# Window attention in units of two images by 64 queries on all 128 rows, with the last four queries of each image apart

## Reference, cut to what matters

```python
    q = (x @ Wq + bq).reshape(B, S, H, hd).transpose(0, 2, 1, 3)
    k = (x @ Wk + bk).reshape(B, S, H, hd).transpose(0, 2, 1, 3)
    v = (x @ Wv + bv).reshape(B, S, H, hd).transpose(0, 2, 1, 3)
    scale = 1.0 / jnp.sqrt(jnp.asarray(hd, x.dtype))
    scores = jnp.einsum('bhqd,bhkd->bhqk', q, k) * scale
    i = jnp.arange(S)[:, None]
    j = jnp.arange(S)[None, :]
    allowed = (j <= i) & (i - j < WINDOW)          # WINDOW = 64
    scores = jnp.where(allowed, scores, NEG_INF)
    attn = jax.nn.softmax(scores, axis=-1)
    out = jnp.einsum('bhqk,bhkd->bhqd', attn, v)
    out = out.transpose(0, 2, 1, 3).reshape(B, S, D)
    return out @ Wo + bo
```

## Time and profile before

| | |
|---|---|
| median of the runs | 1058.24 us |
| the profiled execution | 1058.27 us |
| its span, first to last instruction | 1056.5 us |
| mean granted TensorE clock | 0.961 |
| attention, first scores to last weigh | 54.95 to 222.66 us |
| units in it | 64 |

### The profile page before, as it was taken

How to read it: one execution, slowest core, us unless ns; L and a number is a source line. 1 busy time by engine, 2 the same in 40 slices (tenths; PEclk the granted TensorE clock), 3 DMA queues, 4 the chain that set the end, 5 groups by cost and what they waited for, 6 DMA issues and landing times. The chain is left out here.

```text
span 1056.5 us, 29782 instructions
## 1 busy us (share of the span) xinstructions
PE 950.1 (90%) x10440; PEld 746.9 (71%) x10440; DVE 589.3 (56%) x1463; ACT 412.9 (39%) x1102; POOL 522.1 (49%) x714
## 2 busy tenths in 40 slices
PE   8899999988747999999999999889979947999996
PEld 6667777777634888888888876445546635888895
DVE  1878888865994777433333325678877552111111
ACT  2266776634253344444444422223323222433331
POOL 0056655610604777776777627777773002433332
PEclk9999999999979999999999999989889987999998
DMA  7010000002004988877788723334482046486750
GB/s 257 1 46 2 0 0 0 2 11 75 1 1 165 307 275 254 277 243 224 242 264 255 228 88 100 101 115 120 121 288 82 22 182 228 143 271 215 266 155 26
DMA packets 79821, 149.30 MB, mean 141 GB/s; under 512 B 18892, under 2 KB 53327, under 8 KB 75760
## 3 DMA queue, kind: packets, MB, share of 16 engines
q1 hardware_dynamic: 34768, 77.15, 21.5%
q0 software_dynamic: 17712, 47.88, 15.8%
q10 hardware_dynamic: 27248, 23.09, 6.5%
HBM read 200.22 MB, written 31.73 MB: 220 GB/s over the span
## 5 line engine op out<-in xcount | busy, mean ns | idle before, releaser
L1332 POOL DMA_INDIRECT x_x<-m_x_rows,x_idx x170 | 166.1, 977 | 74.3 <-issue 35.8
L1358 PE MATMUL x_pup<-x_xt,x_w 128*128 128x128 f32 (+1 forms) x2176 | 182.9, 250 | 0.0
L1358 PEld LDWEIGHTS x_pup<-x_xt,x_w 128*128 128x128 f32 (+1 forms) x2176 | 166.9, 165 | 5.9 <-issue 5.7
L1624 POOL DMA_INDIRECT rl_y<-m_y_rows,rl_idx x136 | 134.8, 991 | 43.6 <-issue 37.8
L1439 DVE TENSOR_TENSOR x_hid<-x_gate,x_pup 128x128 f32<-128x128 f32 x170 | 48.9, 288 | 148.2 <-ACT x_gate L1411 142.4
L1372 PE MATMUL x_pdown<-x_w,x_hid 128*128 128x256 f32 (+1 forms) x408 | 104.2, 389 | 0.2 <-DVE x_y L1446 0.2
L1407 ACT ACTIVATE x_xt<-x_pturn 128x256 f32<-128x256 f32 x170 | 65.3, 384 | 89.1 <-PE x_pturn L1343 86.3
L442 POOL TENSOR_TENSOR wa_probs<-wa_probs,wa_peak 68x544 f32<-68x544 f32 x64 | 70.0, 1094 | 57.5 <-DVE wa_peak L593 54.7
L2437 DVE TENSOR_TENSOR x_y<-x_pdown,x_b 128x256 f32<-128x256 f32 x21 | 8.9, 425 | 150.7 <-PE x_pdown L2391 150.7
L2423 ACT ACTIVATE x_hid<-x_pup,x_b 128x128 f32<-128x128 f32 (+1 forms) x200 | 52.8, 357 | 93.7 <-PE x_pup L2374 93.5
L1411 ACT ACTIVATE x_gate<-x_pup 128x128 f32<-128x128 f32 x170 | 47.2, 278 | 92.4 <-PE x_pup L1358 92.4
(11 more groups left out here) (344 smaller groups left out, 1914.8 us busy)
## 6 DMA issues: line engine op xcount, KB each, us to landing
x_w<-in_experts SPq DMA_DIRECT2D x204, 384.0 KB
late_w<-in_w SPq DMA_DIRECT2D x28, 1024.0 KB, 13.3
m_y_rows<-x_y ACTq DMA_DIRECT2D x170, 128.0 KB
xT<-in_w SPq DMA_DIRECT2D x12, 1024.0 KB, 6.1
xn<-in_w SPq DMA_DIRECT2D x10, 1024.0 KB, 10.3
h<-in_w SPq DMA_DIRECT2D x10, 1024.0 KB, 14.0
m_x_rows<-xn SPq DMA_DIRECT2D x34, 128.0 KB, 1.8
x_x<-m_x_rows,x_idx POOLq DMA_INDIRECT x170
```

Source lines behind the costliest of these rows:

```text
L1332: nc.gpsimd.indirect_dma_start(x[:, s, :], None, x_rows, bass.IndirectOffsetOnAxis(ap=idx[:, s:s + 1], axis=0))\
L1358: mm = nc.tensor.matmul(pup[rows:rows + wide, bank, m * P + side * wide:m * P + (side + 1) * wide], w[:, lane, first:first + wide], xt[:, ...
L1624: nc.gpsimd.indirect_dma_start(y[:, t % YR, kk, :], None, y_rows, bass.IndirectOffsetOnAxis(ap=idx[:, n:n + 1], axis=0))\
```

## The change

A unit is now two images and one half of the heads, with the first 64 queries of each: 128 rows (64 of one image, 64 of the other), and 8 heads by 64 keys, 512 columns. There are 32 units, one a step.

- Scores are eight products: for each of the two images four strips of 32 rows, with outputs on rows 0 to 63 or 64 to 127.
- The row sums are taken by DVE from the exponentials (`add_up`, over 512 columns), inverted (8 values a row), and POOL multiplies `probs` by them (`normalise`) ahead of the transposes. The product with ones, the reciprocal over 68 columns and the product behind it are gone.
- Turn is eight full transposes (128 by 128, two heads each); weigh is eight products of 64 columns with all 128 rows.
- The last four queries of both images, with all heads of both halves, make one set of 128 rows per pair of images (every second step). POOL spreads the queries (`last_spread`), TensorE makes four products of 68 columns behind the scores of even steps, ahead of the same `scored`; DVE masks and finds the peak, ACT takes the exponential with its sum, DVE inverts, POOL normalises (`last_normalise`, three instructions), TensorE transposes (`last_turn`), ACT moves, TensorE weighs (`last_weigh`, eight products of 128 columns), DVE picks each row's head (`last_pick`), TensorE sums (`last_sum`), ACT places.
- Values: one job for two images, and one job a block (`vt`) for the values of the last four keys. Queries and keys have two slots, so that a block's projections run during the block before; four projections stand ahead of the first unit.
- Keys are spread two units ahead of their use. POOL in step s does shift(s), normalise(s-1), last_normalise (even) or last_spread (odd), spread(s+2).
- Two products of TensorE that nobody reads stand in each unit: one of 128 columns in `score`, ahead of the wait for the keys, and one of 256 columns in `turn`, ahead of the wait for `normalised`.
- The zeroing of `vals` moves from DVE to POOL; DVE copies the last four tokens' columns of all images (`tails`). Loops are written out in full, without `Fori`. Weight columns of wv are laid out anew and Wo and bv are no longer (in `layout`), ahead of the launch.

The core of the diff:

```diff
-        "mask": np.where((k <= q) & (q - k < WINDOW), 0.0, NEG),
+        "mask": np.where((k2 <= q2) & (q2 - k2 < WINDOW), 0.0, NEG),
+        "last_mask": np.where((k <= HALF + row_query) & (HALF + row_query - k < WINDOW), 0.0, NEG),
+        "head8": (p // HD == np.arange(HC)[None, :]) * 1.0,
+        "row_tail": np.concatenate([(np.arange(8)[None, :] % 4 == 2 * (np.arange(8)[None, :] // 4) + row_image) * 1.0,
+                                    (row_head % 2 == np.arange(2)[None, :]) * 1.0], axis=1),
+        "row_head": (row_head == np.arange(HC)[None, :]) * 1.0,
+        "row_sel": ((sel // 8 == p // 32 % 2) & (sel // 4 % 2 == row_image) & (sel % 4 == row_query)) * 1.0,
...
+    STEPS = B // 2 * DC
+    NPAIR = B // 2
+    LAST = S - HALF
+    LROWS = HC * LAST
...
+        FIRST = [(0, "k0"), (0, "q0"), (0, "k1"), (0, "q1")]
...
+            jobs = [[(blk, "v0"), (blk + 1, "q0")], [(blk, "v1"), (blk + 1, "q1")],
+                    [(blk, "vt"), (blk + 1, "k0")], [(blk + 1, "k1")]][n]
+            return [job for job in jobs if job[0] < NBLK]
...
+                def spread(unit):
+                    c = unit % DC
+                    pool.wait_ge(jobs_moved, done_by(unit, f"k{c}"))
+                    if unit >= 2:
+                        pool.wait_ge(scored, unit - 1)
+                    keys = pair_cols(unit, slice(0, HALF))(kT[:, unit // ABLK % 2, c, :])
+                    for i in range(2):
+                        ins = nc.gpsimd.tensor_tensor(
+                            kheads[:, unit % 2, i, :, :], keys[:, i, :].unsqueeze(1).broadcast_to([P, PER, HALF]),
+                            const("head_of").unsqueeze(2).broadcast_to([P, PER, HALF]), ALU.mult)
+                    ins.then_inc(keys_spread, 1)
+
...
+                def normalise(unit):
+                    pool.wait_ge(inverted, unit + 1)
+                    nc.gpsimd.tensor_tensor(probs[:, unit % 4, :, :], probs[:, unit % 4, :, :],
+                                            inv[:, unit % 2, :].unsqueeze(2).broadcast_to([P, HC, HALF]),
+                                            ALU.mult).then_inc(normalised, 1)
+
...
+                def last_spread(pair):
+                    unit = 2 * pair
+                    pool.wait_ge(jobs_moved, done_by(unit, "q1"))
+                    if pair >= 2:
+                        pool.wait_ge(scored, 2 * (pair - 2) + 1)
+                    for c in range(DC):
+                        queries = pair_cols(unit, slice(HALF, S))(qT[:, unit // ABLK % 2, c, :])
+                        ins = nc.gpsimd.tensor_tensor(
+                            lq[:, pair % 2, c, :, :, :], queries.unsqueeze(2).broadcast_to([P, 2, HC, LAST]),
+                            const("head8").unsqueeze(1).unsqueeze(3).broadcast_to([P, 2, HC, LAST]), ALU.mult)
...
+                def last_normalise(pair):
+                    pool.wait_ge(l_inverted, pair + 1)
+                    if pair:
+                        pool.wait_ge(l_turned, pair)
+                    nc.gpsimd.tensor_tensor(lrows[:, :], const("row_tail"), linv[:, 0:1].broadcast_to([P, 10]), ALU.mult)                        .then_inc(l_rows, 1)
+                    pool.wait_ge(l_rows, pair + 1)
+                    nc.gpsimd.tensor_tensor(ltail[:, :, :], lprob[:, pair % 2, HALF:S].unsqueeze(1).broadcast_to([P, ABLK, LAST]),
+                                            lrows[:, pair % 2 * 4:pair % 2 * 4 + 4].unsqueeze(2)
+                                            .broadcast_to([P, ABLK, LAST]), ALU.mult)
+                    nc.gpsimd.tensor_tensor(lmain[:, :, :], lprob[:, pair % 2, 0:HALF].unsqueeze(1).broadcast_to([P, 2, HALF]),
+                                            lrows[:, 8:10].unsqueeze(2).broadcast_to([P, 2, HALF]),
+                                            ALU.mult).then_inc(l_ready, 1)
...
+                spread(0)
+                spread(1)
+                last_spread(0)
+                for step in range(STEPS + 1):
+                    even = step % 2 == 0
+                    if step < STEPS:
+                        shift(step)
+                    if step >= 1:
+                        normalise(step - 1)
+                    if even and 2 <= step <= STEPS:
+                        last_normalise(step // 2 - 1)
+                    if not even and (step + 1) // 2 < NPAIR:
+                        last_spread((step + 1) // 2)
+                    if step + 2 < STEPS:
+                        spread(step + 2)
...
+                def score(unit):
+                    c, slot = unit % DC, unit // ABLK % 2
+                    pe.wait_ge(jobs_moved, done_by(unit, f"q{c}"))
+                    if unit:
+                        pe.wait_ge(masked, unit)
+                        pe.wait_ge(l_masked, (unit + 1) // 2)
+                    nc.tensor.matmul(pscore[:, 1, 0:P], wq[:, 0, 0:P], wq[:, 1, 0:P], start=True, stop=True)
+                    pe.wait_ge(keys_spread, unit + 1)
+                    queries = pair_cols(unit, slice(0, HALF))(qT[:, slot, c, :])
+                    for i in range(2):
                         for g in range(STRIPS):
                             strip = slice(g * STRIP, (g + 1) * STRIP)
-                            mm = nc.tensor.matmul(pscore[0:S, g, 0:PER * S], qT[strip, c, b * S:(b + 1) * S],
-                                                  kheads[strip, step % 2, :, :].rearrange("p m n -> p (m n)"),
+                            mm = nc.tensor.matmul(pscore[i * HALF:(i + 1) * HALF, g, 0:P], queries[strip, i, :],
+                                                  kheads[strip, unit % 2, i, :, :].rearrange("p m n -> p (m n)"),
                                                   start=True, stop=True)
-                        mm.then_inc(scored, 1)
...
+                def turn(unit):
+                    if unit:
+                        pe.wait_ge(turn_moved, unit)
+                    nc.tensor.matmul(pturn[:, 0:D], wq[:, 0, 0:P], wq[:, 1, :], start=True, stop=True)
+                    pe.wait_ge(normalised, unit + 1)
+                    for two in range(HC // 2):
+                        mm = nc.tensor.transpose(pturn[:, two * P:(two + 1) * P],
+                                                 probs[:, unit % 4, 2 * two:2 * two + 2, :].rearrange("p h n -> p (h n)"), ident)
+                    mm.then_inc(turned, 1)
...
+                    for i in range(2):
+                        for two in range(HC // 2):
+                            mm = nc.tensor.matmul(pout[two * STRIP:(two + 1) * STRIP, i * HALF:(i + 1) * HALF],
+                                                  vals[:, slot, 2 * pair + i, c * (HC // 2) + two, :],
+                                                  probsT[:, unit % 2, two, i, :], start=True, stop=True)
+                    mm.then_inc(weighted, 1)
...
+                def last_turn(pair):
+                    pe.wait_ge(l_ready, pair + 1)
+                    if pair:
+                        pe.wait_ge(l_placed, pair)
+                    nc.tensor.transpose(pl_main, lmain[:, :, :].rearrange("p o n -> p (o n)"), ident)
+                    nc.tensor.transpose(pl_tail, ltail[:, :, :].rearrange("p n q -> p (n q)"), ident).then_inc(l_turned, 1)
...
+                for step in range(STEPS + 3):
+                    jobs = jobs_of(step)
+                    if step < STEPS:
+                        score(step)
+                    if step >= 3:
+                        weigh(step - 3)
+                    if step >= 3 and step % 2 == 1:
+                        last_weigh((step - 3) // 2)
+                    for job in jobs[:1]:
+                        do_job(*job)
+                    if step >= STEPS:
+                        keep_running(3)
+                    if 0 <= step - 2 < STEPS:
+                        turn(step - 2)
+                    for job in jobs[1:]:
+                        do_job(*job)
+                    if 2 <= step < STEPS + 2 and step % 2 == 0:
+                        last_turn(step // 2 - 1)
+                    if step >= 3 and step % 2 == 1:
+                        last_sum((step - 3) // 2)
+                keep_running(3)
...
+                for step in range(STEPS + 3):
+                    even = step % 2 == 0
+                    if step < STEPS:
+                        mask(step)
+                        if even:
+                            last_mask(step // 2)
+                        find_peak(step)
+                        if even:
+                            last_peak(step // 2)
+                    if 1 <= step <= STEPS:
+                        add_up(step - 1)
+                        invert(step - 1)
+                    if even and 2 <= step <= STEPS:
+                        last_invert(step // 2 - 1)
+                    if not even and step >= 3:
+                        last_pick((step - 3) // 2)
...
+                for step in range(STEPS + 4):
+                    even = step % 2 == 0
+                    jobs = jobs_of(step)
```

(54 more changed lines are left out.)

426 lines of the change are left out of this document (197 added, 229 removed).

## The result

| | before | after |
|---|---|---|
| median of the runs | 1058.24 us | 1116.33 us (1101.10 to 1116.65) |
| profiled execution, its span | 1058.27, 1056.5 us | 1116.33, 1114.5 us |
| mean granted TensorE clock | 0.961 | 0.935 |
| attention, first scores to last weigh | 54.95 to 222.66 | 56.03 to 280.02 us |
| from the last weigh to the end of the span | 833.8 us | 834.5 us |

What follows compares the result with a forecast made beforehand. TensorE's issue order would bound the attention stage, with a wait on POOL's chain in even steps. Blocks of 22.1 us against 20.5 and a longer end made it 13 us later: 1058.27 + 13 = 1071 us, range 1052 to 1086.

Steps and rivals of the forecast that it cites:

- What bounds the stage: Attention stage: TensorE's issue order bounds it, with waits for POOL's chain in even steps; other engines add nothing beside this.
- The even step's wait: Before last_turn in even steps: TensorE waits some 1.3 us for POOL's product into lmain, 16 times; step 6.1 us.
- last_weigh at 0.45 us: TensorE's weighing of the last queries in odd steps: all eight products together were taken to cost 0.45 us.
- its block at full clock: Four attention steps: two even at 6.1, odd ones at 5.3 and 4.6, 22.1 us against 20.5 before.
- a wait for last_spread in the short odd steps: Odd steps with one job: last scores wait for POOL's last_spread, ending at 4.2, so scores are done at 4.6 us.
- The first two steps: Steps 0 and 1: no transposes, two jobs sharing one buffer, so job, move, job: 3.8 us each.
- A rival at 0.05: Attention stage: TensorE's waits sum up and its granted clock falls to half; 1095 us or more, chance 0.05.
- the likeliest one: Attention stage: the even-step wait binds, 1060 to 1084 us, time 1071, chance 0.70.
- Scores on eight tiles: Each unit's 16 score instructions of 128 columns on TensorE: 0.45 us, bounds 0.30 and 0.80.
- POOL at 128 rows: POOL's shift and normalise over 512 elements: 1.03 us each, 1.2 at the high end.
- The unread products: Two per unit on TensorE, 0.22 and 0.43 us; the larger covered by the even step's wait, both charged in odd steps.
- The end of the stage: From the last scores' end to the last weigh: 12.3 us, with the last weigh at 235.8.

Runs made afterwards that it cites:

- e8: Changed kernel with last_weigh grouped by row count, last_turn a step later, unread products out, and POOL's last_spread moved to even steps: 1032.2 us.
- e3_turn_later: Changed kernel with last_turn moved into the following odd step behind its first job, last_weigh and last_sum one step later still: 1092.0 us.
- e5_both: Changed kernel with last_weigh grouped by row count and last_turn a step later, unread products kept: 1048.1 us.
- e1_grouped: Changed kernel with last_weigh's four 128-row products first, then its four 16-row products, in place of taking turns: 1073.4 us.
- e4_no_unread: Changed kernel with the two unread products per unit taken out, nothing else: 1102.7 us.
- e7_grouped_no_unread: Changed kernel with last_weigh grouped by row count and the two unread products per unit taken out: 1064.8 us.
- e6_both_no_unread: Changed kernel with last_weigh grouped by row count, last_turn a step later, and the two unread products per unit taken out: 1049.3 us.
- e9_three: Changed kernel with last_weigh grouped by row count, last_turn a step later and last_spread in even steps, unread products kept: 1042.2 us.
- e2_staggered: Changed kernel with last_weigh's eight products ordered value, value, tail, value, tail, value, tail, tail: 1095.1 us.

## Why the prediction was wrong, point by point

- *What bounds the stage.* Right: TensorE's order decides, with the chain to lmain in the even steps; even in e8 POOL is busy 101.54 of 130 us, the vector engine and ScalarE less.
- *The even step's wait.* Right in place and releaser, and nearly in count (15 where 16 was said; the last pair's last_turn did not wait), 4.47 us after the scores where 4.93 was said, step 5.79 where 6.1 was said. e3_turn_later and e5_both show that it costs: taking it away gives 24.4 us alone (18 by the ratios) and 25.3 us on top of e1_grouped.
- *The term that was mis-sized: last_weigh at 0.45 us.* It was priced as sixteen instructions of 128 columns, four tiles at once. But it alternates between 128 rows and 16 rows, and measured 2.65. The price of a change (0.11) was right, and was applied only between functions; the prediction did not look at the row counts of the operands inside one. Each change also ends the overlap of the tiles, so the eight products ran one by one. The Trainium skill, in TensorEngine Tiling (Array Packing), under Key Properties, says that changing the tiling mode drains the engine; it gives no price. The trace agrees: 0.33 us a group, with one product or four in it.
- *With that term near its forecast, the time comes near 1071, in part by luck.* e1_grouped is the changed kernel with last_weigh at 0.68 us, and it takes 1073.4 us. But its block at full clock is 5.79 + 3.76 + 6.30 + 4.86 = 20.7 us where 22.1 was forecast, and a slower start, a slower end and stretches at the lower clock make up for that.
- *The miss in parts.* The last weigh ends at 280.02, forecast 235.8, 44 later. Fourteen last_weighs at 2.20 over their term are 30.8; the lower clock in the steps 21.5; the end 6.6; the start 2.7. The other way, the even steps are 4.6 shorter in all and the rest of the odd steps some 12: transposes counted twice, and a wait for last_spread in the short odd steps that did not come.
- *The first two steps.* 3.8 us each forecast, 4.60 and 4.93 at full clock (e3_turn_later): TensorE's second job waits 0.87 and 2.07 us for ScalarE to move the first one's values out of the buffer. The price of job, move, job was too low.
- *The clock.* A rival at 0.05, with "a wait of 1.59 us left it at 1.00" against it. One wait alone did; a wait of 1.4 us on average (21.7 us in 15) every second step, followed by 2.65 us of single small products, did not. In the profiled execution it cost 21.5 us in the steps and part of the end. So a branch with a chance of 0.05, priced at 1095 or more, came true beside the likeliest one, and the sum had left it out. How much of it falls differs between executions: the one of 1101.10 us had a mean clock of 0.954, the two of 1116 us 0.935 and 0.939.
- *A plain mistake.* The diff transposes two heads with one instruction, four transposes a unit, 0.44 us; the prediction counted eight, 0.88, and the section on the change says eight. The even step hid this (the wait grew by as much), the odd ones were 0.44 shorter than they would have been.
- *Scores on eight tiles.* 0.40 measured (118.39 to 118.79), 0.45 taken.
- *POOL at 128 rows.* 1.042 for 128 x 512, forecast 1.03, high end 1.2. The row of 68 x 544 carried over by elements, though the rows doubled; that of L954 did not. The estimate of 1.1 us from the figure of the Trainium skill (GPSIMD Engine Reference, section 3.1) is 0.07 too high.
- *The unread products.* The prediction charged them in the odd steps and at 0.22 + 0.11 in the even ones. That is some 17 us in all; e4_no_unread and e7_grouped_no_unread gain 13.6 (8.5 by the ratios) and 8.6 us without them, since the clock gives part of it back.
- *The end of the stage.* 18.9 against 12.3: two last_weighs, the first 3.91 us (261.28 to 265.19) since it runs at the lower clock, the second 2.66, and half of the whole at the lower clock. In e5_both it is 10.8.

## What to carry to other kernels

Price a group of small products on TensorE by the changes of tile shape in it, rows as well as columns, not by its columns alone, and order products of one shape together. When a chain through slow engines ends in a step at the end of an engine's list, put that step behind other work of the next round before filling the wait with unread products. Here such products did not pay in any pair of kernels, although they go with a higher clock: without them the time was lower where the waits stood (e4_no_unread, e7_grouped_no_unread), the same in e6_both_no_unread, and 10 us lower where the waits were gone (e8_three_no_unread against e9_three).

## What the runs showed of the hardware

- Between products of 128 rows and of 16 rows on TensorE a group takes 0.33 us at full clock and 0.56 at half, whether it holds one, two or four products of 128 columns on tiles of their own (after, e2_staggered, and 126.45 to 126.78 in e1_grouped).
- The granted clock fell to 0.5 for stretches of some 3 to 10 us (17 in e3_turn_later) although TensorE was busy 117 of 130 us by the records. Busy time did not tell it: in e3_turn_later it was 124 of 130 at 0.97, in e5_both 122 at 1.00. What exactly makes it fall is left open; the runs show only that from 70 to 200 us it stays up with both edits and the unread products (e5_both, e9_three), slips to 0.97 with both edits and without them (e6_both_no_unread), and is back at 1.00 when the wait for last_spread goes too (e8_three_no_unread).
- Consecutive instructions of the vector engine that do not need each other's results start some 0.08 us before the one before ends (119.79 behind 119.18 + 0.69, 119.93 behind 119.79 + 0.22), which is part of the 0.46 us by which the chain was shorter than forecast.
